# The Mamba stage of a fused four-layer kernel: the same result from another split of the work over the engines

## Chip, core and metric

The kernel runs on one core of a Trainium2 chip. The metric is the device time of one launch in microseconds (us). TensorE does the matrix products, VectorE, ScalarE and GpSimd the elementwise work, SyncE issues the loads.

## The reference

The program is four transformer-like layers, each an attention-like part and a feed-forward part behind an adaptive layer norm. Only the first part of the first layer is touched, a Mamba block over x of 16 batches x 256 steps x 128 features. Cut to what matters:

```python
xz = x @ W_in + b_in                          # 128 -> 512
x_proj, z = jnp.split(xz, 2, axis=-1)         # 256 channels each
xa = silu(causal_depthwise_conv(x_proj, conv_k, 4 taps) + conv_b)
dt_int, B_c, C_c = split(xa @ W_xp + b_xp)    # 16, 16, 16
dt = softplus(dt_int @ W_dt + b_dt)
A = -exp(A_log)                               # 256 x 16
h = exp(dt[..., None] * A) * h + dt * B_t * x_t      # a scan over 256 steps, 16 states
y_t = sum(C_t * h, axis=-1)                   # over the 16 states
out = ((y + xa * D_ssm) * silu(z)) @ W_out + b_out
```

## The kernel before

`build_program` runs nine stages one after another on one core, with a barrier between them. `stage_mamba` is the second. Features lie on the partitions, so the 256 channels are CT = 2 tiles of 128 partitions, and the time steps (S = 256) lie along the free axis. All data are fp32.

The stage first does the layer norm of all batches (class `AdaNorm`), and then an item for each of the 16 batches. An item has eight groups g = 0 to 7, and a group treats two of the 16 states for both channel tiles, a tile of 128 x 1024. For a group TensorE spreads the rows B and C of the two states over the partitions (L2643 into `ps_b`, L2647 into `ps_n`, a selecting matrix of 32 rows times `bc`). ScalarE makes `decay` = exp(dt * A) in four instructions of 128x255 (L2723). VectorE makes `drive` = u * B (L2781), runs the recurrence as one scan (L2785, `state`), and multiplies by C (L2792, `read`). TensorE adds the two states of the group and all groups up in PSUM, with two products of 512 columns by the identity (`summed`, L2659, into `ps_y`).

A `phase(n + 1, .., g)` call between the groups of item n prepares the next item: at g = 0 the products with W_in (L2619, L2623), at g = 1 the convolution on VectorE (L2748, L2751), at g = 2 and 3 the gate silu as x / (1 + exp(-x)) with an exponential on ScalarE (L2699) and an addition, a reciprocal and a product on VectorE (L2759, L2761, L2763), at g = 4 the products with W_xp (L2629, L2631), at g = 5 the product with W_dt and the softplus (L2711 to L2716), at g = 6 `dt` and `u` = dt * xa (L2769 to L2776). `back(n - 1)` after group 0 finishes the item before: `y` with the skip term xa * D (L2799), the gate (L2803), the product with W_out (L2669) and the residual (L287, a helper).

The order on each engine is written out by one function, `run`, which every engine calls with its own `group`, `phase` and `back`; each engine works its list strictly in that order, and semaphores hold it where a value isn't there yet. `drive`, `decay`, `read`, `ps_b` and `ps_n` have two buffers, taken in turn by g % 2. GpSimd sets three constants at the start of the stage and does nothing more in it.

The profile counts each fp32 product of TensorE as two MATMUL records, so "x4" in a row of the timeline is two products.

Of the kernel before, what the change touches and what calls it, by code (L numbers as in the profile page):

```python
# [7 lines left out]
P = 128  # L8
ALU = mybir.AluOpType
# [8 lines left out]
GELU = "gelu_and_others"  # L18
SHIFT_A, SCALE_A, GATE_A, SHIFT_B, SCALE_B, GATE_B = range(6)
# [2485 lines left out]
def stage_mamba(core, T):  # L2505
# [9 lines left out]
    G = N // 2  # L2515
    assert CT == 2
    with ExitStack() as ctx:
# [10 lines left out]
        w_xp = sb("w_xp", [P, CT, R + 2 * N])  # L2528
        w_dt = sb("w_dt", [R, CT, P])
# [5 lines left out]
        b_r = sb("b_r", [R, 1])  # L2535
        b_n = sb("b_n", [2 * N, 1])
        A = sb("A", [P, CT, N])
        sel = sb("sel", [2 * N, 2 * N, P])
        one = sb("one", [P, 1])
        xpad = sb("xpad", [P, CT, TAPS - 1 + S])  # L2540
        cz = sb("cz", [P, 2, 4, S])
        sg4 = sb("sg4", [P, 4, S])
        dti = sb("dti", [R, S])
        bc = sb("bc", [2 * N, 2, S])
        soft = sb("soft", [P, CT, S])
        dt = sb("dt", [P, 2, CT, S])
        u = sb("u", [P, 2, CT, 1, S])
        decay = sb("decay", [P, 2, CT, 2, S])
        drive = sb("drive", [P, 2, CT, 2, S])
        state = sb("state", [P, CT, 2, S])  # L2550
        read = sb("read", [P, 2, CT, 2, S])
        y = sb("y", [P, 2, CT, S])
# [9 lines left out]
        LOADS = 12  # L2562
# [4 lines left out]
        def _(sp):  # L2567
            sp.dma_start(w_in[:, :, :], T["L0_attn_W_in"].rearrange("p (t m) -> p t m", m=P)).then_inc(sg["w_in"], 16)
            sp.dma_start(w_xp[:, :, :], T["L0_attn_W_xp"].rearrange("(t p) m -> p t m", p=P)).then_inc(sg["w_in"], 16)
            sp.dma_start(w_dt[:, :, :], T["L0_attn_W_dt"].rearrange("p (t m) -> p t m", m=P)).then_inc(sg["w_in"], 16)  # L2570
            sp.dma_start(w_out[:, :, :], T["L0_attn_W_out"].rearrange("(t p) m -> p t m", p=P)).then_inc(sg["w_in"], 16)
            sp.dma_start(A[:, :, :], T["L0_attn_A_log"].rearrange("(t p) n -> p t n", p=P)).then_inc(sg["w_in"], 16)
            sp.dma_start(sel[:, :, :], T["mamba_sel"]).then_inc(sg["w_in"], 16)
            with nc.allow_non_contiguous_dma("biases"):
# [4 lines left out]
                sp.dma_start(b_r[:, :], T["L0_attn_b_xp"][0:R].rearrange("(p a) -> p a", a=1)).then_inc(sg["w_in"], 16)  # L2579
                sp.dma_start(b_n[:, :], T["L0_attn_b_xp"][R:R + 2 * N].rearrange("(p a) -> p a", a=1)).then_inc(sg["w_in"], 16)  # L2580
# [7 lines left out]
        def run(eng, group, phase, back, finish):  # L2588

            def item(n, j, more=True):  # L2590
                for g in range(G):
                    group(n, j, g)
                    if g == 0 and not (isinstance(n, int) and n == 0):
                        back(n - 1, 1 - j)
                    if more:
                        phase(n + 1, 1 - j, g)

            for g in range(G):
                phase(0, 0, g)
            pairs(eng, B - 2, item)  # L2600
            item(B - 2, 0)
            item(B - 1, 1, more=False)
            back(B - 1, 1)
            finish()

        @block.tensor
        def _(pe):
# [3 lines left out]
            pe.wait_ge(sg["w_in"], 16 * LOADS)  # L2611

            def phase(n, j, g):
                if g == 0:
                    hb = ln.h[:, bass.ds(n, 1), :].rearrange("p b s -> p (b s)")
                    wait(pe, sg["relu"], n)
                    wait(pe, sg["soft_abs"], n)
                    for t in range(2):
                        last = pe.matmul(ps_a[:, t, :], w_in[:, t, :], hb, start=True, stop=True)  # L2619
                    last.then_inc(sg["x_proj"], 1)  # L2620
                    wait(pe, sg["z"], n)
                    for t in range(2):
                        last = pe.matmul(ps_z[:, t, :], w_in[:, 2 + t, :], hb, start=True, stop=True)  # L2623
                    last.then_inc(sg["z_proj"], 1)
                if g == 4:
                    pe.wait_ge(sg["gated"], n + 1)
                    wait(pe, sg["biased"], n - 1)
                    for t in range(CT):
                        pe.matmul(ps_c[0:R, 0, :], w_xp[:, t, 0:R], cz[:, j, t, :], start=(t == 0), stop=(t == CT - 1))  # L2629
                    for t in range(CT):  # L2630
                        last = pe.matmul(ps_c[0:2 * N, 1, :], w_xp[:, t, R:R + 2 * N], cz[:, j, t, :], start=(t == 0), stop=(t == CT - 1))  # L2631
                    last.then_inc(sg["dtbc"], 1)
                if g == 5:
                    pe.wait_ge(sg["dti"], n + 1)
                    for t in range(CT):
                        last = pe.matmul(ps_a[:, t, :], w_dt[:, t, :], dti[:, :], start=True, stop=True)
                    last.then_inc(sg["dt_proj"], 1)

            def group(n, j, g):
                pe.wait_ge(sg["dti"], n + 1)  # L2640
                wait(pe, sg["drive"], G * n + g - 1)
                for k in range(2):
                    last = pe.matmul(ps_b[:, g % 2, 0, k, :], sel[:, 2 * g + k, :], bc[:, j, :], start=True, stop=True)  # L2643
# [397 lines left out]
```

## Time and profile before

| | us |
|---|---|
| time, median of 3 runs | 7111.16 |
| lowest and highest of them | 7107.09, 7113.03 |
| the profiled execution | 7100.05 |
| its span, first to last instruction | 7098.4 |

The trace comes from the profiled execution. The Mamba stage takes from about 36 us to about 1078 us of its span. The granted TensorE clock is given as a share of full speed: 1.00 is 2.4 GHz, 0.50 is 1.2 GHz, and a value between is a mean over a stretch in which both occurred. Busy times count an instruction from its start to its end; products are pipelined, so that their busy time overlaps.

### The profile page before, as it was taken

To read this page: it belongs to the slowest core of one execution; us is meant where nothing else is said; L and a number is where in the kernel's file an instruction comes from. 1 tells how busy PE (TensorE), PEld (TensorE's weight loads), DVE (VectorE), ACT (ScalarE), POOL (GpSimd) and SP (SyncE) were. 2 spreads that over 40 slices of the span, in tenths; PEclk is the share of its full clock that TensorE was granted. 3 is DMA by queue.
4 is the path that set the end of the run, shared out by engine and by line. 5 is a ranking of instruction groups with operands and counts; after the bars stand their busy time and mean duration, and the time that the engine had idled before them with its cause. 6 is when DMAs were issued, how large, how long until landed. Compare 5 with 4: busy or idle time off the path is not lost. (4 is left out here: it accounts for less than half of the span.)

```text
span 7098.4 us, 133197 instructions
## 1 busy us (share of the span) xinstructions
PE 5688.5 (80%) x51841; PEld 3639.4 (51%) x51841; DVE 4735.8 (67%) x7453; ACT 3357.2 (47%) x5656; POOL 2242.4 (32%) x1413
## 2 busy tenths in 40 slices
PE   6878783237978888888888888888889898796866
PEld 3434441114545666666656666666666666564233
DVE  6888885555757667777667767667677777575222
ACT  2323231113545556555655655555565666453123
POOL 0000000000005545545445545445445454362000
PEclk7777776558989999999999999999999999897867
DMA  1000000000000000000000000000000000000000
GB/s 27 0 0 0 0 0 3 0 0 6 2 20 5 5 6 20 5 5 5 21 6 5 18 8 5 5 21 5 5 5 20 6 4 4 8 2 7 0 12 15
DMA packets 53443, 51.26 MB, mean 7 GB/s; under 512 B 17176, under 2 KB 47848, under 8 KB 52080
## 3 DMA queue, kind: packets, MB, share of 16 engines
q1 hardware_dynamic: 44624, 42.67, 2.2%
q8 instruction: 481, 7.88, 0.5%
q10 hardware_dynamic: 8256, 0.03, 0.1%
q14 instruction: 82, 0.67, 0.0%
HBM read 28.03 MB, written 2.10 MB: 4 GB/s over the span
## 5 line engine op out<-in xcount | busy, mean ns | idle before, releaser
L2037 POOL TENSOR_TENSOR lt_qk<-lt_qk,lt_rot 128x1024 f32<-128x1024 f32 x384 | 904.0, 2354 | 633.8 <-DVE lt_rot L2395 633.8
L2086 PE MATMUL lt_ps<-lt_w_qk,lt_xs 128*128 128x512 f32 x1536 | 791.9, 640 | 146.5 <-issue 124.7
L2047 POOL TENSOR_TENSOR lt_prob<-lt_prob,lt_total 128x1024 f32<-128x1024 f32 x192 | 365.1, 1901 | 1261.4 <-DVE lt_total L2421 1261.4
L2042 POOL TENSOR_TENSOR lt_qk<-lt_qk,lt_rnorm 128x1024 f32<-128x1024 f32 x384 | 727.3, 1903 | 63.3 <-ACT lt_rnorm L2271 55.3
L2144 PE MATMUL lt_ps<-lt_z,lt_fold 128*128 128x256 f32 x3072 | 678.8, 379 | 1.1 <-ACT lt_z L2297 1.1
L2144 PEld LDWEIGHTS lt_ps<-lt_z,lt_fold 128*128 128x128 f32 x3072 | 583.6, 190 | 121.4 <-ACT lt_z L2297 24.3
L2392 DVE TENSOR_TENSOR lt_qk<-lt_ps,lt_table 128x1024 f32<-128x1024 f32 x384 | 466.3, 1214 | 263.6 <-ACT lt_sq L2264 259.5
L2264 ACT ACTIVATE lt_sq<-lt_ps 128x1024 f32<-128x1024 f32 x384 | 393.1, 1024 | 469.8 <-PE lt_ps L2086 463.3
L2086 PEld LDWEIGHTS lt_ps<-lt_w_qk,lt_xs 128*128 128x128 f32 x1536 | 269.0, 195 | 440.2 <-issue 394.3
L2395 DVE TENSOR_TENSOR lt_rot<-lt_ps,lt_table 128x512 f32<-128x512 f32 x768 | 489.2, 676 | 0.0
L2411 DVE TENSOR_REDUCE lt_nmax<-lt_ps 128x16 f32<-128x1024 f32 x192 | 235.1, 1225 | 360.0 <-PE lt_ps L2105 360.0
L2402 DVE TENSOR_REDUCE lt_norm<-lt_sq 128x16 f32<-128x1024 f32 x384 | 463.9, 1208 | 0.0
L2659 PE MATMUL mb_ps_y<-mb_read,ident 128*128 128x512 f32 x512 | 367.7, 858 | 97.2 <-DVE mb_read L2792 97.2
L2135 PE MATMUL lt_ps<-lt_probT,lt_xw 64*128 64x256 f32 x3072 | 426.2, 408 | 1.1 <-ACT lt_probT L2287 1.1
L2135 PEld LDWEIGHTS lt_ps<-lt_probT,lt_xw 64*128 64x128 f32 x3072 | 283.3, 194 | 264.2 <-issue 202.3
L2159 PE MATMUL lt_ps<-lt_xn,lt_w 128*128 128x256 f32 (+1 forms) x1152 | 301.8, 399 | 133.5 <-DVE lt_xn L2439 133.5
L2406 DVE TENSOR_SCALAR lt_norm<-lt_norm 128x16 f32<-128x16 f32 x384 | 389.7, 1015 | 13.3
L2297 ACT COPY lt_z<-lt_ps 128x1024 f32<-128x1024 f32 x384 | 379.6, 1014 | 32.9 <-PE lt_ps L2135 17.9
L2093 PE MATMUL lt_ps<-ident,lt_qk 128*128 128x128 f32 x3072 | 372.4, 275 | 4.0 <-POOL lt_qk L2042 4.0
L2093 PEld LDWEIGHTS lt_ps<-ident,lt_qk 128*128 128x128 f32 x3072 | 352.5, 143 | 25.7 <-issue 3.6
L2278 ACT COPY lt_qT<-lt_ps 128x1024 f32<-128x1024 f32 x192 | 194.3, 1012 | 335.6 <-PE lt_ps L2093 335.6
L785 POOL MEMSET fp_wraw<- 128x1120 f32 x1 | 1.0, 1031 | 1039.5 <-POOLq L37 1039.5
(436 smaller groups left out, 11368.8 us busy)
## 6 DMA issues: line engine op xcount, KB each, us to landing
lt_xs<-h SPq DMA_DIRECT2D x96, 64.0 KB, 1.9
lt_w_qk<-in_L_ffn_Wqkv SPq DMA_DIRECT2D x6, 1024.0 KB, 5.2
lt_xs<-h SPq DMA_DIRECT2D x96, 63.8 KB, 2.0
lt_wvT<-in_L_wvT SPq DMA_DIRECT2D x6, 512.0 KB, 7.2
lt_wo<-in_L_ffn_Wo SPq DMA_DIRECT2D x6, 512.0 KB, 8.4
out<-xo SPq DMA_DIRECT2D x8, 256.0 KB, 3.1
lt_w<-in_L_ffn_W SPq DMA_DIRECT2D x6, 341.0 KB, 3.0
wmod<-in_L_wmod SPq DMA_DIRECT2D x4, 384.0 KB, 8.0
```

The source lines that it names most:

```text
L2037: pool.tensor_tensor(qk[:, u, :, :], qk[:, u, :, :], rot[:, u % 2, :, :], ALU.add).then_inc(sg["added"], 1)
L2042: pool.tensor_tensor(qk[:, u, :, :], qk[:, u, :, :], rnorm[:, u, :, :].to_broadcast([P, H, DH]), ALU.mult).then_inc(sg["qk"], 1)
L2086: last = pe.matmul(AT[u][:, 512 * k:512 * k + 512], xs[:, m.j, c:c + P], w_qk[:, a, 512 * k:512 * k + 512], start=True, stop=True)
L2093: last = pe.transpose(to[:, P * g:P * g + P], qk[:, u, 2 * g:2 * g + 2, :].rearrange("p a b -> p (a b)"), core.ident[:, :])
L2135: last = pe.matmul(to[:, c:c + 256], xw[r:r + 64, tile, :], probT[r:r + 64, t, :, WIN * w:WIN * w + WIN], start=True, stop=True, tile_posi ...
L2144: last = pe.matmul(D[:, 0:S], fold[:, slot // 8, slot % 8, :], z[:, k, :, i, :], start=(slot == 0), stop=(slot == H - 1))
L2264: nc.scalar.activation(sq[:, u % 2, :], AT[u], ACT.Square).then_inc(sg["square"], 1)
L2297: act.copy(dst, src.rearrange("p (k c) -> p k c", k=2)).then_inc(sg["z"], 1)
L2392: nc.vector.tensor_tensor(qk[:, u, :, :], src, table[:, t, a, 0, :, :].to_broadcast([P, H, DH]), ALU.mult)
L2395: last = nc.vector.tensor_tensor(rot[:, u % 2, :, HD * k:HD * k + HD], src[:, :, HD * (1 - k):HD * (1 - k) + HD], table[:, t, a, 1, :, HD ...
L2402: nc.vector.tensor_reduce(norm[:, u, :], sq[:, u % 2, :].rearrange("p (h d) -> p h d", h=H), AX.X, ALU.add).then_inc(sg["sumsq"], 1)
L2406: nc.vector.tensor_scalar(norm[:, u, :], norm[:, u, :], 1e-24, None, ALU.max).then_inc(sg["floor"], 1)
```

## The change

GpSimd takes over three products and sums: `drive` (now from `bs`, a copy of B in SBUF, since it reads what ScalarE copies out of PSUM), `both`, the sum of the two states of a group, and `u`. ScalarE copies B for each group (128x512) and computes silu directly, with a switch of its table of functions before and after. TensorE adds one product of 512 columns for each group to `ps_y` in place of two, takes over the convolution (eight products of 256 columns by diagonal matrices `taps`) and the skip term (two products by diagonal `skip`), spreads B and C from separate row tiles (partitions 0 to 31 and 32 to 63 of `sel` and `bcd`), and gets dt, B and C from two products in place of four. VectorE keeps the scan, `read`, the two steps of `dt`, the gate of `y` and the residual. `state` gets a second buffer. GpSimd makes the diagonals once, in ten multiplications of 128x128. The loads are 16 in place of 12. The order of work is written anew: every engine prepares group i + 1 (`ahead`) before it finishes group i - 1 (`here`).

The core of the diff; loads, tile declarations and the removed bodies (which stand above) are left out. LOADS goes from 12 to 16, and N = 16, so BC = 32.

```diff
+        def run(eng, ahead, here, phase, back):
+            def item(n, j, more=True):
+                first = isinstance(n, int) and n == 0
+                for g in range(G):
+                    if g < G - 1:
+                        ahead(n, j, g + 1)
+                    elif more:
+                        ahead(n + 1, 1 - j, 0)
+                    here(n, j, g)
+                    if not first:
+                        back(n - 1, 1 - j, g)
+                    if more:
+                        phase(n + 1, 1 - j, g)
+            for g in range(G - 1):
+                phase(0, 0, g)
+            ahead(0, 0, 0)
+            pairs(eng, B - 2, item)
+            item(B - 2, 0)
+            item(B - 1, 1, more=False)
+            for g in range(4):
+                back(B - 1, 1, g)
 # GpSimd
...
+            def ahead(n, j, g):
+                pool.wait_ge(sg["b_copied"], G * n + g + 1)
+                wait(pool, sg["scanned"], G * n + g - 1)
+                pool.tensor_tensor(drive[:, g % 2, :, :, :], u[:, j, :, :, :].to_broadcast([P, CT, 2, S]),
+                                   bs[:, g % 2, :, :, :].to_broadcast([P, CT, 2, S]), ALU.mult).then_inc(sg["drive"], 1)
+            def phase(n, j, g):
+                if g == 6:
...
+                    pool.tensor_tensor(u[:, j, :, 0, :], dt[:, j, :, :], cz[:, j, 0:CT, :], ALU.mult).then_inc(sg["u"], 1)
+            def added_up(n, j, g):
+                pool.wait_ge(sg["read"], G * n + g + 1)
+                wait(pool, sg["summed"], G * n + g - 1)
+                pool.tensor_tensor(both[:, g % 2, :, :], read[:, g % 2, :, 0, :], read[:, g % 2, :, 1, :], ALU.add).then_inc(sg["both"], 1)
+            def here(n, j, g):
+                if g > 0:
+                    added_up(n, j, g - 1)
+                elif not (isinstance(n, int) and n == 0):
+                    added_up(n - 1, 1 - j, G - 1)
 # TensorE
+            def ahead(n, j, g):
+                if g == 0:
+                    pe.wait_ge(sg["bcd"], n + 1)
+                wait(pe, sg["b_copied"], G * n + g - 1)
+                wait(pe, sg["read"], G * n + g - 1)
+                for k in range(2):
+                    b_last = pe.matmul(ps_b[:, g % 2, 0, k, :], sel[0:BC, 2 * g + k, :], bcd[0:BC, j, :], start=True, stop=True,
+                                       tile_position=(0, 0))
+                    c_last = pe.matmul(ps_n[:, g % 2, 0, k, :], sel[BC:2 * BC, 2 * g + k, :], bcd[BC:2 * BC, j, :], start=True, stop=True,
+                                       tile_position=(BC, 0))
+                b_last.then_inc(sg["b_spread"], 1)
+                c_last.then_inc(sg["c_spread"], 1)
+            def summed(n, j, g):
+                if g == 0:
+                    wait(pe, sg["y_gated"], n)
+                pe.wait_ge(sg["both"], G * n + g + 1)
+                pe.matmul(ps_y[:, :], core.ident[:, :], both[:, g % 2, :, :].rearrange("p t s -> p (t s)"), start=(g == 0),
+                          stop=(g == G - 1)).then_inc(sg["summed"], 1)
+                if g == 0:
+                    for t in range(CT):
+                        pe.matmul(ps_y[:, S * t:S * t + S], skip[:, t, :], cz[:, j, t, :], start=False, stop=False)
...
+            # here(n, j, g) is summed(n, j, g - 1), or summed(n - 1, 1 - j, G - 1) at g = 0
+            # phase: g 0 W_in (4 products), g 1 conv (8), g 3 W_xp (2), g 4 W_dt (2); back: g 1 W_out (2)
+                if g == 1:
+                    pe.wait_ge(sg["x"], n + 1)
+                    for t in range(CT):
+                        for k in range(TAPS):
+                            last = pe.matmul(ps_a[:, t, :], taps[:, k, t, :], xpad[:, t, k:k + S], start=(k == 0), stop=(k == TAPS - 1))
+                    last.then_inc(sg["conv"], 1)
 # ScalarE
+            def ahead(n, j, g):
+                act.wait_ge(sg["b_spread"], G * n + g + 1)
+                wait(act, sg["drive"], G * n + g - 1)
+                act.copy(bs[:, g % 2, 0, :, :], ps_b[:, g % 2, 0, :, :]).then_inc(sg["b_copied"], 1)
...                 # then the four instructions of decay as before
+            # phase: g 0 x; g 2 the following; g 3 bcd; g 4 softplus; back: g 2 tmp
+                if g == 2:
+                    act.preload_act_table_set(SILU)
+                    act.wait_ge(sg["conv"], n + 1)
+                    wait(act, sg["u"], n - 1)
+                    for t in range(CT):
+                        last = nc.scalar.activation(cz[:, j, t, :], ps_a[:, t, :], ACT.Silu, bias=cols[:, 0, t:t + 1])
+                    last.then_inc(sg["silu_x"], 1)
...                 # silu of z in the same way
+                    act.preload_act_table_set(LOG_EXP)
 # VectorE
+            def here(n, j, g):
+                dve.wait_ge(sg["drive"], G * n + g + 1)
+                dve.wait_ge(sg["decay"], G * n + g + 1)
...                 # the scan into state[:, g % 2]
+                dve.wait_ge(sg["c_spread"], G * n + g + 1)
+                wait(dve, sg["both"], G * n + g - 1)
...                 # read, as before; phase: g 5 dt; back: g 0 gate of y, g 3 residual
```

## Rows read from the trace of the kernel before

**Rows 1.** The page: the span of the profiled execution.
```profile
span 7098.4 us, 133197 instructions
```
**Rows 2.** Busy time by stretch: length, each engine's busy us, granted clock.
```profile
98.00:1034.00 936.00, 749.06 (x1801) 384.02 (x1800) 800.40 (x647) 287.92 (x663) 0.00 (x0) 0.72 0.00 0
75.00:98.00 23.00, 9.65 (x22) 5.48 (x23) 13.45 (x14) 5.77 (x12) 0.00 (x0) 0.57 0.00 0
1150.00:1500.00 350.00, 107.47 (x276) 61.33 (x276) 201.10 (x369) 56.40 (x117) 4.80 (x12) 0.59 0.00 0
```
**Rows 3.** Groups of instructions from 98 to 1074 us, by form.
```profile
L2785 DVE TENSOR_TENSOR_SCAN mb_state<-mb_decay,mb_drive 128x1024 f32<-128x1024 f32 x128 | 293.3, 2292 | 29.5 <-ACT mb_decay L2723 25.6
L2723 ACT ACTIVATE mb_decay<-mb_dt,mb_A 128x255 f32<-128x255 f32 x511 | 213.0, 494 | 83.0 <-DVE mb_dt L2773 55.0 <-DVE mb_state L2785 27.9
...
L2792 DVE TENSOR_TENSOR mb_read<-mb_state,mb_ps_n 128x1024 f32<-128x1024 f32 x128 | 156.2, 1221 | 5.4
L2781 DVE TENSOR_TENSOR mb_drive<-mb_u,mb_ps_b 128x1024 f32<-128x1024 f32 x128 | 155.7, 1216 | 98.2 <-PE mb_ps_b L2643 97.4
...
L2761 DVE RECIPROCAL mb_sg<-mb_sg 128x1024 f32<-128x1024 f32 x15 | 98.3, 6553 | 0.5
```
**Rows 4.** VectorE's timeline (start, length): the convolution of item 1 and of item 15.
```profile
107.90 0.73 DVE L2748 TENSOR_SCALAR mb_cz<-mb_xpad,mb_kern,mb_cols 128x256 f32<-128x256 f32 x2
...
981.93 0.73 DVE L2748 TENSOR_SCALAR mb_cz<-mb_xpad,mb_kern,mb_cols 128x256 f32<-128x256 f32 x2
```
**Rows 5.** TensorE's timeline at full clock (513 us) and at half (557 us).
```profile
513.35 1.02 PE L2643 MATMUL mb_ps_b<-mb_bc,mb_sel 32*128 32x256 f32 x4
...
514.22 1.02 PE L2647 MATMUL mb_ps_n<-mb_bc,mb_sel 32*128 32x256 f32 x4
...
557.68 2.07 PE L2643 MATMUL mb_ps_b<-mb_bc,mb_sel 32*128 32x256 f32 x4
559.55 1.91 PE L2647 MATMUL mb_ps_n<-mb_bc,mb_sel 32*128 32x256 f32 x4
```
**Rows 6.** TensorE's timeline: the sum of the last item's last group.
```profile
1070.53 2.46 PE L2659 MATMUL mb_ps_y<-mb_read,ident 128*128 128x512 f32 x4 [2.73 <-DVE mb_read L2792]
```
**Rows 7.** GpSimd's groups of instructions in later stages, by form.
```profile
L2037 POOL TENSOR_TENSOR lt_qk<-lt_qk,lt_rot 128x1024 f32<-128x1024 f32 x384 | 904.0, 2354 | 633.8 <-DVE lt_rot L2395 633.8
L2042 POOL TENSOR_TENSOR lt_qk<-lt_qk,lt_rnorm 128x1024 f32<-128x1024 f32 x384 | 727.3, 1903 | 63.3 <-ACT lt_rnorm L2271 55.3
...
L1014 POOL TENSOR_TENSOR gq_k_raw<-gq_k_raw,gq_rope 128x512 f32<-128x512 f32 x64 | 81.0, 1266 | 61.6 <-ACT gq_k_raw L1176 61.6
```
**Rows 8.** ScalarE's copy of 512 columns out of PSUM, by form.
```profile
L2936 ACT COPY mo_gatesT<-mo_ps_r 8x512 f32 x6 | 3.4, 574 | 12.9 <-PE mo_ps_r L2894 12.9
```
**Rows 9.** TensorE's timeline: products of 32 rows in different row tiles, first and last.
```profile
1801.82 0.48 PE L1403 MATMUL df_ps_s<-df_k,df_q 32*128 32x256 f32 x2
...
1802.59 0.38 PE L1417 MATMUL df_ps_st<-df_q,df_k 32*128 32x256 f32 x2
```
**Rows 10.** Timeline at 3008 us: a hand-over from ScalarE to GpSimd.
```profile
3007.98 0.21 ACT L2271 ACTIVATE lt_rnorm<-lt_log 128x16 f32<-128x16 f32 x1
...
3008.34 1.90 POOL L2042 TENSOR_TENSOR lt_qk<-lt_qk,lt_rnorm 128x1024 f32<-128x1024 f32 x1 [0.56 <-ACT lt_rnorm L2271]
```
**Rows 11.** Timeline at 3014 us: ScalarE's table of functions is switched.
```profile
3014.22 1.28 ACT L2360 ACT_TABLE_LOAD   x1
3015.52 1.19 ACT L2321 ACTIVATE lt_gel<-lt_ps,lt_vecs 128x256 f32<-128x256 f32 x3
```
**Rows 12.** Timelines: the residual beside GpSimd (6166 us) and with GpSimd idle (1032 us).
```profile
6166.06 0.77 POOL L1024 TENSOR_SCALAR_AFFINE_SELECT gq_prob<-gq_prob 128x256 f32<-128x256 f32 x2 [0.52 <-ACT gq_prob L1185]
...
6166.48 0.62 DVE L287 SCALAR_TENSOR_TENSOR x<-gq_tmp,mod,x 128x256 f32<-128x256 f32 x1
...
1032.51 0.48 DVE L287 SCALAR_TENSOR_TENSOR x<-mb_tmp,mod,x 128x256 f32<-128x256 f32 x1
```
**Rows 13.** VectorE's timeline: the first group's drive.
```profile
97.93 1.22 DVE L2781 TENSOR_TENSOR mb_drive<-mb_u,mb_ps_b 128x1024 f32<-128x1024 f32 x1
```

More of the change, by code:

```diff
@@ L2515, in stage_mamba @@
     G = N // 2
-    assert CT == 2
+    BC = 2 * N
+    assert CT == 2 and BC == 32
     with ExitStack() as ctx:
@@ L2586, in _ @@
             pool.memset(decay[:, :, :, :, :], 0.0).then_inc(sg["const"], 1)
[L2588 to L2604, printed above, removed]
+            pool.wait_ge(sg["w_in"], 16 * LOADS)
@@ L2606, in _, with back @@
+            def here(n, j, g):
[3 more added lines that the diff above has]
+                    added_up(n - 1, 1 - j, G - 1)
+            def back(n, j, g):
+                if isinstance(n, int) and n == B - 1 and g == 0:
+                    added_up(n, j, G - 1)
+            run(pool, ahead, here, phase, back)
         @block.tensor
@@ L2611, in _ @@
             pe.wait_ge(sg["w_in"], 16 * LOADS)
-            def phase(n, j, g):
+            pe.wait_ge(sg["diagonals"], 1)
+            def ahead(n, j, g):
                 if g == 0:
[L2615 to L2643, printed above, removed]
-                last.then_inc(sg["b_spread"], 1)
+                    pe.wait_ge(sg["bcd"], n + 1)
+                wait(pe, sg["b_copied"], G * n + g - 1)
                 wait(pe, sg["read"], G * n + g - 1)
@@ L2663, in back @@
-            def back(n, j):
-                if isinstance(n, int) and n == B - 1:
-                    summed(n, j, G - 1)
-                pe.wait_ge(sg["y_gated"], n + 1)
-                wait(pe, sg["dti"], n + 2 if not (isinstance(n, int) and n == B - 1) else 0)
-                for t in range(CT):
-                    last = pe.matmul(ps_c[:, 0, :], w_out[:, t, :], y[:, j, t, :], start=(t == 0), stop=(t == CT - 1))
-                last.then_inc(sg["out"], 1)
-            run(pe, group, phase, back, lambda: None)
+                    wait(pe, sg["relu"], n)
@@ new lines, in back @@
+            def back(n, j, g):
+                if isinstance(n, int) and n == B - 1 and g == 0:
+                    summed(n, j, G - 1)
+                if g == 1:
+                    pe.wait_ge(sg["y_gated"], n + 1)
+                    pe.wait_ge(sg["bcd"], n + 1 if isinstance(n, int) and n == B - 1 else n + 2)
+                    for t in range(CT):
+                        last = pe.matmul(ps_c[:, 0, :], w_out[:, t, :], y[:, j, t, :], start=(t == 0), stop=(t == CT - 1))
+                    last.then_inc(sg["out"], 1)
@@ L2674, in _ @@
+            run(pe, ahead, here, phase, back)
         @block.scalar
@@ L2818, in stage_moe @@
+            run(dve, lambda n, j, g: None, here, phase, back)
 def stage_moe(core, T):
```

202 lines of the change are left out of this document (90 added, 112 removed).

## The prediction

> **What bounds the kernel now.** I read the page first, for the span [rows 1], then the busy time by stretch. The Mamba stage is the only part that the change touches, and in its steady part VectorE is busy 800 of 936 us and TensorE 749 [rows 2]. So VectorE is the nearest bound, with TensorE close behind. The groups of instructions say what VectorE does: drive, scan and read take 1.22 + 2.29 + 1.22 = 4.73 us a group, and the reciprocal of the gate 6.55 us an item; VectorE waits 97 us in all for `ps_b` [rows 3], since TensorE is late with the spread when it comes back from other work. The timeline gives the period: (981.93 - 107.90) / 14 = 62.4 us an item [rows 4]. The first drive starts at 97.9 [rows 13], so the last item starts at 97.9 + 15 x 62.4 = 1034, and its last sum at 1070.5 [rows 6]: without phases an item takes 36.5 us.
>
> TensorE's price depends on its clock. Two products of 256 columns follow each other by 0.87 us at full clock and by 1.87 us at half [rows 5]. I take 0.44 and 0.92 us for 256 columns, and twice that for 512. The mean clock of the stage is 0.72 [rows 2].
>
> **What the change does to each engine.** VectorE loses drive, the convolution, the reciprocal with its neighbours, u and the skip term. It keeps 2.29 + 1.22 = 3.51 us a group [rows 3], 28 us an item, and a few small steps, so about 31 of the 54 us that it is busy in an item now. TensorE saves 512 columns a group and gains 2560 columns an item (eight products of the convolution and two of the skip). ScalarE gains a copy of B a group, about 0.58 us by the row of 512 columns out of PSUM [rows 8], to 1.66 us of decay (213.0 us / 128) [rows 3]. GpSimd gains drive, both and u. No engine is full by this. What counts is the order in which each waits for the others.
>
> **The loop that the new order makes.** Write i for the group in hand. Every engine calls ahead(i + 1) first and here(i) after it:
>
> - TensorE: spread(i + 1), then summed(i - 1), then the phase's products, then spread(i + 2).
> - ScalarE: copy(i + 1) once spread(i + 1) is there.
> - GpSimd: drive(i + 1) once copy(i + 1) is there, and only then both(i - 1).
> - TensorE's summed(i - 1) waits for both(i - 1), and spread(i + 2) stands behind it.
>
> both(i - 1) needs only read(i - 1), which is long there, but it stands behind drive(i + 1) in GpSimd's list, and drive(i + 1) waits for TensorE. So spread, copy, drive, both and summed follow one another once for every group, and nothing of one turn overlaps the next. Behind summed on TensorE stand the phase's products, so they add to the loop too; behind drive on GpSimd stands both, and TensorE waits for that.
>
> **The price of a turn.**
>
> - drive on GpSimd, 128x1024: no row has this form. The sum of two full tiles takes 2.35 us, the product with a value repeated along the inner axis 1.90 us [rows 7]. drive reads two full inner rows of 256, so it is nearest to the first: 2.35.
> - both, 128x512: 1.27, by a product of this size [rows 7].
> - copy: 0.58 [rows 8].
> - spread: four products of 256 columns, B and C in different row tiles. Elsewhere 16 records, eight products, in different row tiles take 1802.59 + 0.38 - 1801.82 = 1.15 us [rows 9], 0.14 us each in place of 0.44. With two tiles I take a factor of two: as long as two products now, 1.02 us at full clock and 1.95 at half [rows 5]. The lower bound is this; the upper bound is no overlap, three products before B's last one is out, about 1.5 and 2.85.
> - summed: 0.88 at full, 1.84 at half.
> - hand-overs: four. From ScalarE to GpSimd one takes 3008.34 - 3008.19 = 0.15 us [rows 10], the others I take as less; 0.3 us together.
>
> Full clock: 1.02 + 0.58 + 2.35 + 1.27 + 0.88 + 0.3 = 6.4 us a group. Half: 1.95 + 0.58 + 2.35 + 1.27 + 1.84 + 0.3 = 8.3 us. The other engines fit: scan and read take 3.5 us from the end of drive(i), decay ends 1.7 us after copy, before drive's 2.35.
>
> The phases: W_in 4, convolution 8, W_xp 2, W_dt 2, W_out 2, skip 2, so 20 products of 256 columns, 8.8 us at full clock and 18.4 at half. An item then takes 8 x 6.4 + 8.8 = 60.0 us at full and 8 x 8.3 + 18.4 = 84.8 at half; the last one, without phases, 51.2 and 66.4.
>
> Costed at nothing: u (1.27 us on GpSimd) lies beside summed, spread and copy, at least 2.5 us; without that cover it adds 16 x 1.27 = 20 us. The diagonals, ten small products on GpSimd, lie under the layer norm; four more loads too, since the layer norm lasts until 71 us. Prologue and tail: a reciprocal of 6.55 us goes, the convolution on TensorE, and u and drive on GpSimd, come. I put -3 us.
>
> The table switches: two loads of 1.28 us, and the next instruction starts 0.02 us after the load ends [rows 11]. In phase 2 ScalarE then has decay 1.7, two loads 2.6 and four silu of about 0.42 each, 1.7: 6.0 us against a turn less its copy, 5.8 at full and 7.7 at half. Nothing at half, 0.2 us an item at full. The Trainium skill (ScalarE: Activation LUTs, What ACT_TABLE_LOAD costs) adds a drain of about 1.38 us to each switch. By it the stall would be 1.0 to 3.0 us an item, an estimate of 15 to 45 us more in all; the trace has no such gap behind a load, so the sum goes without it.
>
> **The clock.** Now TensorE is busy 80% at a mean of 0.72. Where it is busy 42% the clock is 0.57, and 31% goes with 0.59 [rows 2]. In the new loop it works in one piece of 3.8 us (half clock) and then sits idle for 4.5 us; its busy share is (8 x 3.8 + 18.4) / 84.8 = 57% at half and 40% at full. Between the rows that gives about 0.63, so full clock in a share of 0.26 of the time. Then an item takes 1 / (0.26 / 60.0 + 0.74 / 84.8) = 76.6 us, and the last 1 / (0.26 / 51.2 + 0.74 / 66.4) = 61.7.
>
> **The sum.** 15 x (76.6 - 62.4) + (61.7 - 36.5) - 3 = 213 + 25 - 3 = +235 us on the profiled execution of 7100.05 us, whose span is 7098.4. The median of the runs shown, 7111.2, is 11 us above it. So 7346 us, 3.3% slower.
>
> The terms at their ends: clock 0.57 gives 7402, clock 0.72 gives 7270. drive at 1.90 takes off 128 x 0.45 = 58 us: 7288, and with clock 0.72 about 7212. No overlap of the row tiles adds about 0.8 x 128 = 102: 7448.
>
> **Rivals.**
>
> *GpSimd is held up by the scan.* In a later stage the residual on VectorE, with both inputs in SBUF, takes 0.62 us beside GpSimd and 0.48 without it. It ends at 6167.10, which is 0.27 us (256 columns) after GpSimd's end at 6166.83 [rows 12]: as if its reading began only when GpSimd was done. The scan has two SBUF inputs, and scan(i) and both(i - 2) become ready at the same moment, the end of drive(i). If GpSimd is first, the scan waits 1.3 us, which the loop doesn't feel. If the scan is first and holds both up, each turn grows by about 2.2 us: 128 x 2.2 = 282, 7628 us. GpSimd needs no semaphore from another engine at that point, so I hold it to be first more often. The Trainium skill (SBUF, State Buffer, Who interferes with whom) states that a VectorE instruction with two SBUF inputs contends with a GpSimd instruction that reads SBUF, and that issue order decides who blocks; rows 12 agree with it.
>
> *The clock stays up.* If the loop runs at full clock throughout, the sum is 15 x (60.0 - 62.4) + (51.2 - 36.5) - 3 = -24: 7087 us, faster. It takes a mean clock of about 0.96 to break even. Against it: at 80% busy the clock is 0.72.
>
> *The loop doesn't bind.* If both went before drive, or overlapped it, the busiest engine would set the pace: TensorE at half clock, 8 x 3.8 + 18.4 = 49 us an item. 15 x (49 - 62.4) and 6 less in the last item give about 6905. Nothing in the lists of work allows it.
>
> **Chances.** The loop as costed, 0.60. The scan ahead of GpSimd, 0.20. No overlap of the row tiles, 0.10. The clock stays up, 0.06 (half of it near enough to before to count as the same). The loop doesn't bind, 0.04. The range of 7235 to 7640 leaves out the last two and some of the ends of the first. A difference under 0.2% can't be told from no change here: slower 0.90, same 0.03, faster 0.07.
>
> **What the profile after would show.** The stage longer by some 235 us; spread, copy, drive, both and summed each starting within 0.1 us of the end of the one before; summed's idle time put down to `mb_both`, and drive's to `mb_bs`; both at 1.27 us if GpSimd isn't held up, and at over 3 us or starting late if it is; VectorE busy near half of the stage, waiting for `mb_drive`; the clock near 0.6. Two runs of records from `ps_b` and `ps_n` start together if the row tiles overlap. I am wrong if the period is under 62 us, or if both and drive are found to be much shorter than 3.6 us together.

## The result and the profile after

The changed kernel takes 7351.3 us (median of 4 runs, 7343.5 to 7354.8), the kernel before 7109.1 in the same comparison: ratio 1.0341, 95% interval 1.0324 to 1.0359. The forecast was 7346, from a difference of 235 us. The medians differ by 242 us and the spans of the two profiled executions by 254.7. The first view is the busy time of the stretch of [rows 2], with the same columns:

```profile
98.00:1034.00 936.00, 490.36 (x1427) 255.23 (x1426) 452.73 (x250) 302.96 (x645) 383.09 (x204) 0.59 0.00 0
```

No engine is busy more than 52% of the time; before, VectorE had 86% [rows 2]. So what costs the time is waiting, and the clock fell from 0.72 to 0.59. The groups of the whole stage (90 to 1330 us) say who waits for whom:

```profile
L2810 DVE TENSOR_TENSOR_SCAN mb_state<-mb_decay,mb_drive 128x1024 f32<-128x1024 f32 x128 | 409.7, 3201 | 484.9 <-POOL mb_drive L2630 481.1 <-ACT mb_decay L2754 3.8
L2630 POOL TENSOR_TENSOR mb_drive<-mb_u,mb_bs 128x1024 f32<-128x1024 f32 x128 | 303.1, 2368 | 727.2 <-ACT mb_bs L2748 722.1 <-issue 5.0
L2682 PE MATMUL mb_ps_y<-mb_both,ident 128*128 128x512 f32 x256 | 264.7, 1138 | 584.0 <-POOL mb_both L2643 584.0
...
L2643 POOL TENSOR_TENSOR mb_both<-mb_read 128x512 f32<-128x512 f32 x128 | 163.8, 1280 | 0.3 <-DVE mb_read L2817 0.3
...
L2748 ACT COPY mb_bs<-mb_ps_b 128x512 f32<-128x512 f32 x127 | 74.1, 583 | 572.9 <-PE mb_ps_b L2671 572.9
```

Read the last column as a ring: the scan waits for `drive`, `drive` for the copy, the copy for TensorE's `ps_b`, TensorE for `both`, and `both` waits for nobody (0.3 us), since it stands right behind `drive`. Each link waits over 480 us. `drive` and scan were 1.22 and 2.29 us before [rows 3]; now they are 2.37 and 3.20. One turn of the ring in the timeline (start, length, engine):

```profile
505.18 0.59 ACT L2748 COPY mb_bs<-mb_ps_b 128x512 f32<-128x512 f32 x1 [11.97 <-PE mb_ps_b L2671]
...
505.84 2.35 POOL L2630 TENSOR_TENSOR mb_drive<-mb_u,mb_bs 128x1024 f32<-128x1024 f32 x1 [10.59 <-ACT mb_bs L2748]
...
507.74 1.28 ACT L2765 ACT_TABLE_LOAD   x1
508.14 1.26 POOL L2643 TENSOR_TENSOR mb_both<-mb_read 128x512 f32<-128x512 f32 x1
508.22 3.33 DVE L2810 TENSOR_TENSOR_SCAN mb_state<-mb_decay,mb_drive 128x1024 f32<-128x1024 f32 x1 [9.57 <-POOL mb_drive L2630]
509.03 0.84 ACT L2769 ACTIVATE mb_cz<-mb_ps_a,mb_cols 128x256 f32<-128x256 f32 x2
...
509.46 2.07 PE L2682 MATMUL mb_ps_y<-mb_both,ident 128*128 128x512 f32 x2 [4.31 <-POOL mb_both L2643]
...
511.46 0.79 PE L2671 MATMUL mb_ps_b<-mb_bcd,mb_sel 32*128 32x256 f32 x1
...
511.47 0.79 PE L2673 MATMUL mb_ps_n<-mb_bcd,mb_sel 32*128 32x256 f32 x1
...
512.90 0.63 PE L2671 MATMUL mb_ps_b<-mb_bcd,mb_sel 32*128 32x256 f32 x1
...
513.57 0.59 ACT L2748 COPY mb_bs<-mb_ps_b 128x512 f32<-128x512 f32 x1 [1.67 <-PE mb_ps_b L2671]
```

From copy to copy it takes 8.39 us, with TensorE at half clock. No link overlaps the next by more than 0.07 us. The tile `both` and the last sum (shortest, median and longest in ns, then the first and the last start):

```profile
L2682 PE MATMUL mb_ps_y<-mb_both,ident x256: 1057/1061/1222, 104.1 to 1327.4; 128*128 128x512 f32 x128
L2643 POOL TENSOR_TENSOR mb_both<-mb_read x128: 1251/1265/3261, 102.7 to 1324.9; 128x512 f32<-128x512 f32 x128
```

The same row of the kernel before, for the place of its last sum:

```profile
L2659 PE MATMUL mb_ps_y<-mb_read,ident x512: 592/872/1223, 104.8 to 1071.9; 128*128 128x512 f32 x171
```

The last sum starts at 1327.4 against 1071.9, 255.5 us later, and the whole span is 254.7 us longer: the loss lies in the Mamba stage. This split, the last sum and the rest of the span behind it, is used for every run below.

### The profile page after: what moved, and what is told of

It reads as the page before. It is cut to its first block and busy times, and to the rows that moved or that the text cites. A ratio compares the mean times of both kernels' runs of the same rounds, so it can differ in the third digit from the quotient of the medians.

```text
span 7353.1 us, 133394 instructions
## 1 busy us (share of the span) xinstructions
PE 5524.4 (75%) x51649; PEld 3576.6 (49%) x51841; DVE 4492.9 (61%) x7101; ACT 3456.5 (47%) x5816; POOL 2759.0 (38%) x1695
## 5 line engine op out<-in xcount | busy, mean ns | idle before, releaser
L2810 DVE TENSOR_TENSOR_SCAN mb_state<-mb_decay,mb_drive 128x1024 f32<-128x1024 f32 x128 | 409.7, 3201 | 484.9 <-POOL mb_drive L2630 481.1
L2682 PE MATMUL mb_ps_y<-mb_both,ident 128*128 128x512 f32 x256 | 264.7, 1138 | 584.0 <-POOL mb_both L2643 584.0
L2630 POOL TENSOR_TENSOR mb_drive<-mb_u,mb_bs 128x1024 f32<-128x1024 f32 x128 | 303.1, 2368 | 727.2 <-ACT mb_bs L2748 722.1
L2682 PEld LDWEIGHTS mb_ps_y<-mb_both,ident 128*128 128x128 f32 x256 | 64.2, 311 | 662.7 <-POOL mb_both L2643 589.6
```

Source lines behind the costliest of these rows:

```text
L2810: nc.vector.tensor_tensor_scan(state[:, g % 2, :, :, :].rearrange("p a b s -> p (a b s)"), decay[:, g % 2, :, :, :].rearrange("p a b s -> ...
```

## Experiments

| kernel | time, us | ratio to before | clock, 98 to 650 | last sum | rest |
|---|---|---|---|---|---|
| before | 7109.1 | 1 | 0.73 | 1071.9 | 6026.5 |
| changed | 7351.3 | 1.0341 | 0.59 | 1327.4 | 6025.7 |
| e1 both ahead of drive | 6902.0 | 0.9701 | 0.67 | 867.4 | 6029.6 |
| e2 sum read directly | 6772.5 | 0.9525 | 0.89 | 798.8 | 5950.2 |
| e3 addition twice | 7742.1 | 1.0886 | 0.57 | 1702.3 | 6036.9 |
| e4 useless products | 7108.7 | 0.9995 | 0.77 | 1200.1 | 5902.0 |
| e5 only the addition | 7195.8 | 1.0120 | 0.56 | 1115.3 | 6083.3 |
| e6 drive back, sum direct | 6708.9 | 0.9441 | 0.91 | 742.1 | 5980.3 |
| e7 drive back | 6770.9 | 0.9532 | 0.74 | 744.5 | 6014.5 |
| e8 e5 and products | 7213.1 | 1.0154 | 0.62 | 1199.1 | 6012.1 |
| e9 u back | 7352.4 | 1.0357 | 0.58 | 1329.7 | 6012.8 |
| e10 changed, 96 products | 7264.6 | 1.0237 | 0.60 | 1359.5 | 5895.8 |
| e11 before, 96 products | 7006.7 | 0.9870 | 0.72 | 1111.7 | 5896.1 |
| e12 e6, 96 products | 6774.8 | 0.9545 | 0.89 | 780.0 | 5993.9 |

Half widths of the intervals of the ratios are 0.0013 to 0.0025. Each ratio is to the kernel before as it was measured beside that run (7096.8 to 7111.4 us). Last sum and rest are of one execution each, the profiled one, and are in us; the clock is that of the stretch from 98 to 650 us.

**e1, is it the order on GpSimd?** Only GpSimd's list changes, so that `both(i - 1)` no longer stands behind `drive(i + 1)`.

```diff
...
                 for g in range(G):
+                    if here_first:
+                        here(n, j, g)
                     if g < G - 1:
...
-                    here(n, j, g)
+                    if not here_first:
+                        here(n, j, g)
...
-            run(pool, ahead, here, phase, back)
+            run(pool, ahead, here, phase, back, here_first=True)
```

> The changed kernel, with one edit: in GpSimd's list both(i - 1) stands before drive(i + 1), not behind it. Theory of the loop: both no longer waits for TensorE's spread, so summed can be done while copy and drive run. What is left is a chain over two turns, spread, copy, drive, scan, read: 1.95 + 0.58 + 2.35 + 3.3 + 1.2 + 0.4 = 9.8 us for two groups at half clock, 4.9 a group, and some 10 to 18 us of phases an item: 49 to 57 us an item in place of about 77. That gives 6970 us, between 6880 and 7080. Rival, GpSimd's instructions or their collisions with the scan cost by themselves: the same work in another order, so less than 1% from 7351.

Measured: 6902, 449 us below the changed kernel and 3% below the kernel before, with the same instructions. The last sum comes 460 us sooner. This is the ring, cut. It was worth more than the 381 us that I gave it, though 6902 lies in the range.

**e2, is it `both` at all?** GpSimd adds nothing; TensorE sums `read` in two products, as before.

```diff
-                pe.wait_ge(sg["both"], G * n + g + 1)
-                pe.matmul(ps_y[:, :], core.ident[:, :], both[:, g % 2, :, :].rearrange("p t s -> p (t s)"), start=(g == 0),
-                          stop=(g == G - 1)).then_inc(sg["summed"], 1)
+                pe.wait_ge(sg["read"], G * n + g + 1)
+                for k in range(2):
+                    last = pe.matmul(ps_y[:, :], core.ident[:, :], read[:, g % 2, :, k, :], start=(g == 0 and k == 0),
+                                     stop=(g == G - 1 and k == 1))
+                last.then_inc(sg["summed"], 1)
...                 # added_up on GpSimd is empty; read on VectorE waits for summed in place of both
```

> The changed kernel without both: TensorE adds read up itself by two products of 512 columns, as in the kernel before; all else as changed. Theory of the loop: summed waits for read alone, which is long there. The chain over two turns is 8.8 us at half clock, 4.4 a group; TensorE has 5.6 us a group at half clock, 2.8 at full, and is denser, so the clock rises. 45 to 55 us an item: 6900 us, between 6800 and 7050, though TensorE multiplies twice the columns for the sum. The scan back at 2.29 us. Rival, the clock: if TensorE's time a turn is what matters, the added 128 products of 512 columns cost 110 to 235 us: 7460 to 7590.

Measured: 6772, 579 us below the changed kernel, and below my range of 6800 to 7050. TensorE has twice the columns in the sum and the clock is 0.89. The addition that was to spare TensorE work makes the kernel slow where it stands: without it the last sum comes 529 us sooner, and with it ahead of `drive` (e1) 460. 76 us of the gain are in the rest of the span, in code that is the same (see e10); without them the time is in the range.

**e3, what does a microsecond on the ring cost?** The addition is made a second time, into a tile that nobody reads.

```diff
...                 # a tile again, of the shape of both
+                pool.tensor_tensor(again[:, g % 2, :, :], read[:, g % 2, :, 0, :], read[:, g % 2, :, 1, :], ALU.add)
                 pool.tensor_tensor(both[:, g % 2, :, :], read[:, g % 2, :, 0, :], read[:, g % 2, :, 1, :], ALU.add).then_inc(sg["both"], 1)
```

> The changed kernel, with the addition of the two states made twice on GpSimd (the first time into a tile of its own that nobody reads). Theory of the loop: both lies on the path in full, so 128 x 1.27 = +163 us, 7514 us, and a little more if the clock falls. Rival, GpSimd has slack of which 1.3 us a group can be used: within 0.5% of 7351.

Measured: 391 us more than the changed kernel, where I expected 163; 375 us of it are in the stage, 2.9 a group, not 1.27. The timeline says why:

```profile
508.31 1.26 POOL L2644 TENSOR_TENSOR mb_again<-mb_read 128x512 f32<-128x512 f32 x1
508.38 3.33 DVE L2812 TENSOR_TENSOR_SCAN mb_state<-mb_decay,mb_drive 128x1024 f32<-128x1024 f32 x1 [3.55 <-POOL mb_drive L2631]
509.53 3.24 POOL L2645 TENSOR_TENSOR mb_both<-mb_read 128x512 f32<-128x512 f32 x1
```

The first addition started before the scan and takes 1.26; the scan then takes 3.33 in place of 2.29. The second addition starts inside the scan and takes 3.24 in place of 1.27: it ends after the scan does. So each holds the other up, and the one that starts second pays. That is the mechanism of my rival "GpSimd is held up by the scan". In the changed kernel it did not happen, where GpSimd starts 0.08 us sooner (508.14 against 508.22): of its 128 `both` only the last one takes 3.26 us. The Trainium skill (SBUF, State Buffer, Who interferes with whom) says that issue order decides who blocks; these rows agree, in both directions.

**e4, what is the clock worth?** Two useless products of 512 columns a group on TensorE, between B's and C's spread; B's semaphore goes up ahead of them, so that the ring itself does not get longer.

```diff
...                 # B's two products
+                b_last.then_inc(sg["b_spread"], 1)
+                for k in range(2):
+                    pe.matmul(ps_n[:, g % 2, 0, :, :].rearrange("p k s -> p (k s)"), core.ident[:, :], taps[:, :, 0, :], start=True, stop=True)
...                 # C's two products
```

> The changed kernel, with two products of 512 columns of no use between the spread of B and that of C, into the buffer that C's spread then overwrites. They lie beside copy, drive and both (4.5 us) and are there to keep TensorE at work. It leaves out the overlap of B's and C's row tiles. If the clock rises to 0.9 or above, a turn falls from 8.3 towards 6.4 us and an item from 77 to 61 to 64: 7110 to 7170 us. If it stays at 0.6, the two products and C's spread take 5.6 us at half clock, 1.1 more than they have, and the time rises by up to 128 x 1.1 = 140 us to 7490. The first is what the theory of the loop with a price for the clock expects.

Measured: 7108.7, 243 us faster than the changed kernel with more work. But the split says that only 127 us of the profiled 251 lie in the stage, where the clock rose from 0.59 to 0.77. The other 124 lie behind it, where nothing was changed. So 7108.7, just below the range of my first branch (7110 to 7170), is no hit: it wanted the clock at 0.9 and the whole gain in the stage. I first put all of it down to the clock, and e10 showed that to be wrong. What the clock is worth on the ring itself can be read here: between 1176.91 and 1183.41 one turn, from copy to copy, is at full clock. It takes 6.50 us (forecast 6.4), against 8.39 at half.

```profile
1176.91:1183.41 6.50, 5.15 (x15) 2.30 (x15) 4.18 (x3) 2.18 (x5) 3.57 (x2) 1.00 0.00 1
```

**e5 and e8, the addition by itself.** The kernel before, with its old order, and only the addition on GpSimd; e8 adds one useless product of 512 columns a group, into the half of `ps_n` that C's spread then overwrites.

```diff
...
+            def group(n, j, g):
+                pool.wait_ge(sg["read"], G * n + g + 1)
+                wait(pool, sg["summed"], G * n + g - 1)
+                pool.tensor_tensor(both[:, g % 2, :, :], read[:, g % 2, :, 0, :], read[:, g % 2, :, 1, :], ALU.add).then_inc(sg["both"], 1)
...                 # summed as in the changed kernel; the next product in e8 alone
+                pe.matmul(ps_n[:, g % 2, 0, :, :].rearrange("p k s -> p (k s)"), core.ident[:, :],
+                          ln.h[:, 0:2, :].rearrange("p b s -> p (b s)"), start=True, stop=True)
```

> The kernel before, with one part of the change alone: GpSimd adds the two states of a group (both), and TensorE adds one product of 512 columns in place of two. The order of work is the old one, in which nothing stands ahead of both on GpSimd. Theory of the loop: no loop arises. both starts when read ends and lies beside drive, which has one input in SBUF, so it is nearly done when the scan starts. TensorE saves 512 columns a group, which can take away part of VectorE's 97 us of waits for the spread, and the sum comes 0.4 us later. 7080 us, between 7040 and 7130. Rival, the addition on GpSimd costs by itself: 128 x 1.27 = +160 us or more, 7270.

> The kernel before with only the addition of a group's two states on GpSimd (as in e5), and one useless product of 512 columns a group more on TensorE, into the diagonal half of ps_n before C's spread overwrites it, so that TensorE has as many columns a group as the kernel before. It adds work to the engine and nothing else, and the output is the reference's. Theory 1, e5 was slow because TensorE's granted clock sat at 0.56 and not 0.73 in an item: with the columns back the clock returns to 0.70 or more and the time falls below e5's 7195.8, to about 7110 (7080 to 7150); the scan still takes 2.3 to 3.3 us beside GpSimd, so it is no gain on the kernel before. Theory 2, e5 was slow because GpSimd's addition holds up VectorE (1.3 us a group at the shared memory) and the clock only went along: then the clock may rise but the time stays at 7190 or above; and if the extra product itself is on the path, 0.43 us a group more, 7195 plus 55, 7250.

e5 missed: I expected 7080 and it took 7195.8. In the stage it loses 43.4 us, behind the stage 56.8. The kernel before has a mean clock of 0.73 in its items. This is e5's busy time in its last item and the end of the one before it, between 1040 and 1110 us:

```profile
1040.00:1110.00 70.00, 65.36 (x118) 35.26 (x118) 55.32 (x42) 21.65 (x51) 13.91 (x11) 0.50 0.00 0
```

TensorE works nearly without a gap (65.36 of 70 us) and stays at its lower level of 1.2 GHz, so that a group takes 5.71 us (the sums at 1098.22, 1103.93 and 1109.65). With 512 columns less a group TensorE became the bound there. In the items the period is 64.7 us in place of 62.4. Part of it are instructions of VectorE that meet the addition. The first step of the convolution, two instructions, takes 1.68 us in place of 0.73 an item (14 us in all), one of the two being held up to 1.36 us. e8's theory 1 fell: with the columns given back the clock is 0.62, not 0.73, TensorE is busy 481 of 552 us, and the last sum comes 84 us later than in e5, 0.65 us a group, so the added product is on the path. That the whole time rises by only 17 us is again the rest, 71 us shorter. Theory 2 had the time, at 7190 or above, but not this split. Why the clock does not come back with the same columns is not settled.

**e6 and e7, `drive` on VectorE again**, out of PSUM and without the copy; e7 keeps the addition on GpSimd, e6 sums directly as e2 does.

```diff
+                dve.wait_ge(sg["b_spread"], G * n + g + 1)
+                dve.wait_ge(sg["u"], n + 1)
+                nc.vector.tensor_tensor(drive[:, g % 2, :, :, :], u[:, j, :, :, :].to_broadcast([P, CT, 2, S]),
+                                        ps_b[:, g % 2, :, :, :].to_broadcast([P, CT, 2, S]), ALU.mult).then_inc(sg["drive"], 1)
...                 # GpSimd's drive and ScalarE's copy are gone; TensorE waits for drive in place of the copy
```

> The changed kernel with drive on VectorE from PSUM, as in the kernel before, no copy of B, and the sum of read made on TensorE by two products of 512 columns: GpSimd keeps u alone. Theory: VectorE sets the pace, 8 x 4.73 + 3 = 41 us an item and some waits, 45 against 62.4 before: 6840 us, between 6780 and 6950. If it comes near to e2 (6772), the change's gain is the convolution, the silu and the skip term taken off VectorE, and drive on GpSimd gives nothing more.

> As e6, but the two states are added on GpSimd (both), as in the changed kernel and in its order. drive isn't in GpSimd's list, so both waits for read alone, and the loop is gone. 6840 us, within 60 of e6. Rival, the addition on GpSimd costs by itself in the new order: 100 us or more above e6.

e6 is the fastest of all, 5.6% below the kernel before (6708.9 against 7102.5 beside it), and 71 us below my range. Its busy time:

```profile
98.00:650.00 552.00, 486.54 (x1853) 265.71 (x1852) 535.76 (x392) 290.06 (x626) 16.55 (x13) 0.91 0.00 0
```

VectorE is busy 97% of the time: now it is the bound. An item takes 40.8 us in place of 62.4. Some 14 us of the difference are work that left VectorE (53.4 us busy an item before, 39.6 now: the convolution, the reciprocal with its neighbours, `u` and the skip term), and some 8 us are waits that are gone (9.0 before, 1.2 now). e7's last sum is 2.4 us behind e6's: with no ring, the addition on GpSimd hardly touches the stage. Of the 37 us between the two profiled spans, 34 are in the rest. The medians are 62 us apart, just over the 60 that I allowed and short of the rival's 100; e6's profiled execution was the slowest of its four, e7's the fastest.

**e9, is `u` free?** `u` goes back to VectorE.

```diff
...
-                    pool.tensor_tensor(u[:, j, :, 0, :], dt[:, j, :, :], cz[:, j, 0:CT, :], ALU.mult).then_inc(sg["u"], 1)
+                    nc.vector.tensor_tensor(u[:, j, :, 0, :], dt[:, j, :, :], cz[:, j, 0:CT, :], ALU.mult).then_inc(sg["u"], 1)
```

> The changed kernel with u = dt * x on VectorE again, right behind dt's last product, as in the kernel before; nothing else. Prediction's step: u on GpSimd costs and saves nothing, since it is made an item ahead; 7351 within 0.3% (7330 to 7373). Rival: u on GpSimd, 3.26 us as measured beside the scan, sits in the loop through GpSimd once an item: then 15 x 3.3 = 49 us come back and the kernel takes 7302 or less.

Measured: 7352.4, no difference; the step holds at the clock of the changed kernel. In e4, with the faster turns, `drive` waits for `u` in 8 of the items, 2.0 us in all, so there the cover is just used up.

**e10 to e12, what moves the rest?** Behind the Mamba stage all kernels have the same code, yet the rest goes from 5902 to 6083 us in the runs so far. Each of these three adds 96 small products, made once, ahead of the Mamba stage.

```diff
+            for k in range(96):
+                pe.matmul(ps_a[:, 0, 0:16], core.ident[:, :], core.ident[:, 0:16], start=True, stop=True)
```

> The changed kernel with 96 small useless products (16 columns each, into ps_a before it is first written) on TensorE, once, between the layer norm and the Mamba stage; nothing else. What it asks: e4 was 249 us faster than the changed kernel, of its profiled span 127 us from the last Mamba sum on backwards and 124 us after that sum, in stages whose code nobody touched and whose granted clock is 0.98 either way; there TensorE has fewer short idle times that no other engine ends. Over all profiles so far the time from the last sum to the end falls with the number of TensorE products written out in the Mamba code: 316 products (e5) 6083 us, 364 (before, e8) 6026 and 6012, 376 (changed, e1, e3, e7, e9) 6013 to 6037, 424 (e2, e6) 5950 and 5980, 472 (e4) 5902. Theory A, it is where the later code lies in TensorE's instruction stream: with 96 more it is where e4 had it, the last sum stays at 1327 (plus up to 12 us for the products), the rest falls to about 5902 and the time is 7240 (7210 to 7275). Theory B, it is what e4 did in the Mamba stage (a state of the clock or of the queues carried over): the rest stays at 6013 to 6037 and the time is 7345 to 7365.

> The kernel before with the same 96 small useless products once ahead of its Mamba stage. Theory A of e10: 364 + 96 = 460 products, by the line through the others some 5915 us after the last sum in place of 6026, so 7000 (6970 to 7040), faster than the kernel before for no reason of its own. Theory B: 7100 to 7120.

> The fastest version so far (e6: drive on VectorE, the sum directly from read's output, convolution and skip term on TensorE, reciprocal on the others as in the changed kernel), with the same 96 products ahead. It has 424 + 96 = 520. Theory A: the rest falls from 5980 to 5850 to 5930 if the fall goes on with the number, and the time to 6580 to 6660; if the effect comes round again (a matter of where a loop's ends fall), it can be back at 6700 or above. Theory B: 6709 plus at most 10.

Theory B falls. e10's rest is 5895.8 and e11's 5896.1, 130 us below their bases, as in e4, while the stage keeps its length: e10's first sum is at 136.7, 32.6 us later than the 104.1 above, and its last one 32.1 later. The granted clock of the rest is 0.91 in the changed kernel and in e10. The added products cost those 32 us, more than the 12 that I allowed, so the time is 7264.6 and not 7240. The kernel before with 96 useless products is 1.3% faster than without.

The texts on record have 316 products for e5, 364 for the kernel before and e8, and 460 for e11, which is 12 too few. Counted in the code, with the 16 products of the layer norm, the number is 328 in e5, 376 in the kernel before, the changed kernel, e1, e3, e7, e8 and e9, 424 in e2 and e6, 472 in e4, e10 and e11, and 520 in e12. By this count the three kernels with 472 have rests of 5896 to 5902 us, though their stages end between 1112 and 1360 us and e4's added products run in every group. That speaks for the place of the later code and against a mere delay of it. The seven with 376 have 6012 to 6037 and the two with 424 have 5950 and 5980, so a difference of up to 30 us isn't read from the rest alone.

e12 missed Theory A's 5850 to 5930: its rest is 5993.9, 13.6 us longer than e6's, and with the 38 us of the added products its span is 51.5 us longer (the medians are 66 apart). So it is not "the more, the faster". My other branch, that the effect comes round again, could hardly have failed. Of the waits of TensorE behind the stage (wait, us in total, times, longest) this one differs most. For the changed kernel:

```profile
PE lt_ps L2087 <- issue: 131.1, 40, 6.7
```

and for e10:

```profile
PE lt_ps L2087 <- issue: 41.0, 10, 6.6
```

then for e6 and for e12:

```profile
PE lt_ps L2087 <- issue: 109.6, 32, 6.7
...
PE lt_ps L2087 <- issue: 122.1, 40, 6.5
```

"issue" is idle time that nothing shown in the profile ends. It falls by 90 of the 130 us in e10 and rises by 12.5 of the 13.6 us in e12, at the same line in the same code. So it is shown that the added instructions make the difference. That it is by the place of the later instructions in TensorE's stream is the reading that fits best, and not shown: no run moved that place alone. That the cause is the loading of instructions is my guess; no view shows it.

## Why the prediction was right, step by step

**The ring.** Right, link by link, forecast in brackets: copy 0.59 us (0.58), `drive` 2.35 (2.35), `both` 1.26 (1.27), from the start of the sum to the spread 2.00 (1.84), spread 2.07 (1.95). The gaps are 0.07 us from copy to `drive`, 0.06 from `both` to the sum and 0.04 from spread to copy, and `both` starts 0.05 before the recorded end of `drive`; I had put 0.3 in all. The turn is 8.39 us at half clock (8.3), and 6.50 at full clock in e4 (6.4). e1 shows that the order on GpSimd makes it. The row tiles overlap: the records of L2671 and L2673 start 0.01 us apart.

**The clock.** The stage ran at 0.59, where I took 0.63. By my own formula that is a share of 0.18 at full clock and an item of 1 / (0.18 / 60.0 + 0.82 / 84.8) = 78.9 us. This is the term that was most off in size. The convolution of item 1 starts at 107.62 and that of item 14 at 1128.52, so an item takes 1020.90 / 13 = 78.5 us; forecast 76.6.

That the formula comes so near is in part luck, since the clock did not mix as it assumes. I let whole turns run at full clock for a quarter of the time. None does: the shortest of the 256 records of the sum is 1.057 us, which is half clock. TensorE comes up to full clock only behind the products of the phases, as in the convolution, whose eight products take 3.62 us.

The turns of the item from 726.51 us on take 14.21, 8.40, 8.76, 10.63, 8.59, 8.48, 8.47 and 10.99 us. Eight turns of 8.4 are 67.2, and the phases add 11.3. My 76.6 was 8 x 7.7 = 61.7 for the turns and 14.9 for the phases. The first was 5.5 too low, the second 3.6 too high. In the second, two more things went against each other. W_dt's products run beside the spread and cost nothing (L2721 starts 0.01 us before L2671 at 764.17). The softplus on ScalarE, which I had not costed, stands ahead of the copy: in the turn of 10.63 us the spread is done at 766.25 and the copy starts at 768.51.

```profile
757.88 0.59 ACT L2748 COPY mb_bs<-mb_ps_b 128x512 f32<-128x512 f32 x1 [0.58 <-PE mb_ps_b L2671]
...
764.17 0.79 PE L2721 MATMUL mb_ps_a<-mb_bcd,mb_w_dt 16*128 16x256 f32 x1
764.18 0.79 PE L2671 MATMUL mb_ps_b<-mb_bcd,mb_sel 32*128 32x256 f32 x1
...
766.35 0.84 ACT L2784 ACTIVATE mb_soft<-mb_ps_a,mb_cols 128x256 f32<-128x256 f32 x2 [6.29 <-PE mb_ps_a L2721]
767.22 0.63 ACT L2787 ACTIVATE mb_soft<-mb_soft 128x512 f32<-128x512 f32 x1
...
767.88 0.72 ACT L2789 ACTIVATE mb_soft<-mb_soft,mb_one 128x512 f32<-128x512 f32 x1
768.51 0.56 ACT L2748 COPY mb_bs<-mb_ps_b 128x512 f32<-128x512 f32 x1
```

Two sums of the last item, one turn apart:

```profile
1304.71 2.08 PE L2682 MATMUL mb_ps_y<-mb_both,ident 128*128 128x512 f32 x2 [4.32 <-POOL mb_both L2643]
...
1313.10 2.08 PE L2682 MATMUL mb_ps_y<-mb_both,ident 128*128 128x512 f32 x2 [4.31 <-POOL mb_both L2643]
```

**The sum.** The first `drive` starts at 89.5 in place of 97.9: -8.4 (forecast -3). 15 x (78.5 - 62.4) = +241.5 (forecast +213). The last item takes 1327.4 - (89.5 + 15 x 78.5) = 60.4, against 1071.9 - 1034 = 37.9: +22.5 (forecast +25), its turns 8.39 apart in the rows just above. Together +255.6, against 255.5 read from the last sums. The forecast of +235 was too low by 1.9 us an item, 28 us, less 5 for the prologue and 3 for the last item. The stage was 20 us longer than forecast, yet the median came out only 5 us above 7346. That is luck too: the profiled execution of the kernel before was 9 us below its median and that of the changed kernel 3.5 above, so the medians lie 12 us closer than the spans.

**What was costed at nothing.** `u`: takes 3.26 us beside the scan and not 1.27, still hidden (e9). Table loads: the next instruction starts at 509.03, 0.01 us after 507.74 + 1.28; no gap behind it, as in [rows 11], and the estimate of 15 to 45 us more, which rested on a drain behind each load, does not come true. The scan at 3.33: not on the ring, as forecast, since it starts when `both` does and ends long before the next `drive`.

**Rivals.** "GpSimd is held up by the scan" would have cost 282 us, 2.2 a turn; e3 shows the price to be real, an addition of 3.24 us in place of 1.27. It hangs on 0.08 us. "The clock stays up" is not what happens, but its premise is right that the clock matters: e4 gets 127 us of the stage back net of its own products. "The loop doesn't bind" was given 6905; e1, which unbinds it, takes 6902, though by other terms than mine: `drive` runs inside the scan there and takes up to 4.33 us, and the clock is 0.67.

**What I left out.** The time behind the stage. It was 6026.5 and 6025.7 in the two kernels, so it cancelled; both happen to have 376 products written out, which nobody planned. e5 and e10 show +57 and -130 us for -48 and +96 of them. With another number the same reasoning could have missed by more than half of the 235 us. The range did not cover that, and should have: 7351 less 130 is 7221, below its lower end of 7235.

## What to carry to other kernels

Write out, for each engine, what stands ahead of the instruction that another one waits for; two harmless orders can close into a ring that no engine's busy time shows. Here one swap in one queue was worth 6%. Work saved on an engine that is not the bound bought nothing here, and where TensorE had less to do its clock was lower (e5, 0.56 against 0.73). Before crediting an edit with a gain of 1 or 2%, split the span at the end of the edited stage: if stages that nobody touched moved, the gain is not the edit's.

## What the runs showed that I had not expected

- A scan and an addition or product on GpSimd delay each other by nearly the whole of what is left of the first: scan 2.29 to 3.33 us, addition 1.27 to 3.24, `u` 1.27 to 3.26, `drive` on GpSimd 2.35 to 4.33 (e1).
- Granted clock 0.50 over 70 us in which TensorE was busy 93% (e5); 0.62 at 87% busy (e8), against 0.73 at 80% in the kernel before. Busy time alone does not tell the clock.
- Unchanged code behind the edit runs up to 187 us shorter or longer (5896 to 6083), as TensorE instructions are added ahead of it or taken away; with the same number it differs by up to 30 us.
